# Output projection as split products, y2 reloaded in parts, and half of the last residual on TensorE, in a vision tower kernel on one core

## The chip, the cores and the metric

The kernel runs on one core of a Trainium2 chip. The metric is device time in microseconds of one execution, lower is better; a kernel's time is the median of its runs. The profile shows TensorE (PE, its weight loads PEld), VectorE (DVE), ScalarE (ACT), GpSimd (POOL) and SyncE (SP), which issues most DMAs; ScalarE issues the others. TensorE's clock has two levels here, 1.2 GHz (0.50 in the profile) and 2.4 GHz (1.00).

## The reference

64 images of 3x224x224 are cut into 16x16 patches, 196 tokens each, and embedded to D = 192. The embedding is regrouped for the heads; the rest is one block, all in f32:

```
h   = embed(x)                                       # (64, 196, 192)
q,k,v = silu(h Wq), silu(h Wk), silu(h Wv)           # 12 heads of 16
a   = (q k^T * decay) v ;  a = a * sigmoid(h Wg1 Wg2)
o   = layernorm(a Wo) * ln_w + ln_b
h2  = layernorm(h + o)
xn  = rms_norm(h2) * norm_w ; tok = l2norm(xn) ; sl = l2norm(slots) * scale
L   = sl tok^T ; dispatch = softmax over tokens, combine = softmax over slots
y   = fc2(gelu(fc1(dispatch xn)))                    # 64 slots, each its own 192x768x192
out = layernorm(h2 + combine y)
```

## The kernel before

Two images make an item: NP = 32 items of PT = 392 tokens, in tiles of T = 98 tokens, four a item. There are three stages, each a loop written once for every engine; the engines meet in semaphores alone, and each engine works in program order.

**Stage one, phase1(step)**, runs 34 steps; step i works on the front part of item i (`a`: embedding, q, k, v, gate, scores, values), the middle of item i-1 (`c`: output projection, norms, residual) and the end of item i-2 (`d`: logits, softmaxes, slot inputs, combine weights). The last two steps (NP and NP+1) have no `a`: the drain. Products that need f32 accuracy are done in one of two ways: as plain f32 matmuls (two records each in the profile), or by `product` (L914 to L916) as three matmuls of fp32r operands, each operand split beforehand into a rounded part and the rest. The embedding, q, k and v are split that way; `project_out` (L944) is plain f32 from `og` (attention output times gate, written by VectorE in `gated`, L784) and `wo`. In a step TensorE does embed(i, 0), project_out(i-1, 0), token_features(i-2), embed(i, 1), project_out(i-1, 1), then the rest. VectorE's first_norm starts with bn_stats on the projection's bank (L717). ScalarE starts a step with second_norm (h2, L600), then turned_h (hT, L605, and hTh, L607), and later squares gn into `sq` for a sum (L583). SyncE's step loads the x of item i+2 (after GpSimd's last split of the x before), then stores h2 of item i-2 and the combine weights.

**Stage two, phase2**, runs 32 slot pairs: fc1 (L1191 to L1200), gelu on ScalarE (L636), turns of it (L1209), fc2 (L1178), VectorE's copies hgT (L873) and y2st (L879), ScalarE's store of y2 to DRAM (L643). Six weight buffers are refilled by SyncE as they come free. Behind its last weight loads SyncE issues the first four loads of cbuf (combine weights) and h2r (h2), and then reads y2 back as `y2r`, [128, 32, 192]: rows of slots 0 to 51 of both halves as soon as these are stored, slots 52 to 59 next, slots 60 to 63 last, six DMAs (L377).

**Stage three, phase3**, runs 32 output steps on four sets of buffers (DEEP = 4): GpSimd adds the bias (y2b, L513), TensorE makes four products of 64 rows (L1224) into two PSUM banks, VectorE adds h2r to all four tiles (res, L887), takes statistics (L893, L896), and after GpSimd's power (L508, L510; out_rstd) makes nb3 of the step before (L902, shift); ScalarE writes the four output tiles (L653) from res and issues the store (L656). SyncE reloads cbuf and h2r four steps ahead.

## Time and profile before

| | |
|---|---|
| median of 3 runs | 1304.57 us (1303.42 to 1306.14) |
| the profiled execution's own time | 1307.93 us |
| its span, first to last instruction | 1306.2 us |
| mean granted clock | 0.947 |
| PE busy | 1200.2 us (92%) |
| DVE busy | 782.9 us (60%) |
| ACT busy | 708.3 us (54%) |
| POOL busy | 572.3 us (44%) |
| chain that ended last | PE 74%, DVE 16%, issue 5% |

The shares of busy time are means over the three stages. The page's 40 slices (32.7 us each) show stage one up to slice 30, stage two up to slice 36, and stage three in the last four; the granted clock is below full speed in the first slice, at the change from stage one to stage two, and from the end of stage two on. A busy TensorE is one that has a matmul in flight; ends are modelled.

### The profile page before, as it was taken

How to read it: one execution, taken by the hardware profiler on the slowest of the kernel's cores; microseconds unless marked ns; L12 is line 12 of the kernel's file. 1: busy time of each engine (PE TensorE's matmuls, PEld its weight loads, DVE VectorE, ACT ScalarE, POOL GpSimd, SP SyncE). 2: the span in 40 equal slices, each digit the busy share in tenths (PEclk: the TensorE clock that was granted, in tenths of full speed). 3: DMA queues.
4: the chain of work that ended last, by engine and by line, in shares of the span. 5: the costliest groups of instructions: out<-in, count | busy, mean ns of one | idle time of the engine just before them, and what ended most of it. 6: DMA issues, size and time to landing. Idle time of an engine off the chain costs nothing.

```text
span 1306.2 us, 34037 instructions
## 1 busy us (share of the span) xinstructions
PE 1200.2 (92%) x12578; PEld 962.2 (74%) x12578; DVE 782.9 (60%) x2049; ACT 708.3 (54%) x1613; POOL 572.3 (44%) x878
## 2 busy tenths in 40 slices
PE   5999999999999999999999999999996999995553
PEld 4788888888888888888888888888873555553332
DVE  4566666666666666666666666666673222221797
ACT  5456666666666666666666666666653111110476
POOL 4355454555545554545555455545442000000564
PEclk8999999999999999999999999999995999998655
DMA  4411211111111112111111111121071899995686
GB/s 140 183 39 60 79 61 49 49 49 49 49 49 49 49 57 77 63 49 49 49 49 49 49 49 49 57 78 62 13 270 58 352 422 420 421 389 124 190 263 188
DMA packets 50246, 158.33 MB, mean 121 GB/s; under 512 B 5292, under 2 KB 31266, under 8 KB 37794
## 3 DMA queue, kind: packets, MB, share of 16 engines
q1 hardware_dynamic: 32610, 145.04, 30.9%
q10 hardware_dynamic: 17600, 12.78, 3.2%
q8 instruction: 26, 0.43, 0.1%
q14 instruction: 10, 0.08, 0.0%
HBM read 132.18 MB, written 25.62 MB: 121 GB/s over the span
## 4 chain that ended last, share of the span: by engine, by line
PE 74%; DVE 16%; issue 5%; ACT 1%; POOL 1%; DVEq 1%; SPq 1%; DMA 0%; ACTq 0%; POOLq 0%
PE ps L914 9%; PE ps L915 8%; PE ps L916 7%; DVE p_sb L778 7%; PE ps L973 7%; PE ps L944 6%; PE ps L1008 6%; PE ps L1178 5%; PE ps L1195 4%; PE ps L1051 3%; PE ps L956 3%; PE ps L957 2%; DVE res L887 2%; PE ps L991 2%; PE ps L1074 2%
## 5 line engine op out<-in xcount | busy, mean ns | idle before, releaser
L413 POOL TENSOR_TENSOR xl<-x_sb,xh 128x392 fp32r<-128x392 f32 x192 | 189.1, 1019 | 86.6 <-DVE gn L753 78.7
L778 DVE TENSOR_TENSOR p_sb<-ps,dec 98x1176 f32<-98x1176 f32 x128 | 177.0, 1383 | 56.4 <-PE ps L973 56.4
L973 PE MATMUL ps<-qm,kT 32*98 32x196 f32 x1536 | 117.0, 343 | 9.7 <-DVE p_sb L778 7.6
L717 DVE BATCH_NORM_STATS2 st<-ps 98x6 f32<-98x192 f32 x128 | 40.0, 355 | 130.8 <-PE ps L944 130.8
L1008 PE MATMUL ps<-p_sb,vpad 98*32 98x98 f32 x3072 | 112.7, 251 | 1.5 <-DVE p_sb L778 1.5
L636 ACT ACTIVATE hg<-ps 128x768 f32<-128x768 f32 x32 | 26.0, 812 | 159.0 <-PE ps L1200 159.0
L1008 PEld LDWEIGHTS ps<-p_sb,vpad 98*32 98x32 f32 x3072 | 84.7, 109 | 35.0 <-issue 24.6
L973 PEld LDWEIGHTS ps<-qm,kT 32*98 32x98 f32 x1536 | 75.2, 158 | 35.2 <-DVE p_sb L778 23.1
L944 PE MATMUL ps<-wo,og 96*98 96x192 f32 x512 | 93.7, 325 | 0.0
L879 DVE COPY y2st<-ps 128x192 f32<-128x192 f32 x32 | 11.4, 358 | 136.1 <-PE ps L1178 128.7
L1224 PE MATMUL ps<-y2b,cbuf 64*98 64x192 f32 x256 | 48.2, 526 | 44.6 <-POOL y2b L513 44.6
L653 ACT ACTIVATE o_sb<-res,nb,rstd 98x192 f32<-98x192 f32 x128 | 59.6, 536 | 54.4 <-DVE nb L902 53.7
L944 PEld LDWEIGHTS ps<-wo,og 96*98 96x98 f32 x512 | 83.2, 164 | 0.9
L457 POOL TENSOR_TENSOR invn<-nrm,expo 98x4 f32<-98x4 f32 x32 | 32.4, 1011 | 117.6 <-DVE nrm L763 117.6
L914 PE MATMUL ps<-xl,wh 128*128 128x392 f32 x192 | 70.3, 366 | 11.8 <-POOL xl L413 11.8
L500 POOL CAST pickb<-pick 128x128 fp32r (+1 forms) x32 | 9.4, 293 | 162.4 <-PE ps L1200 162.4
L443 POOL TENSOR_TENSOR qd<-qs,qdec 96x196 f32<-96x196 f32 x64 | 36.0, 563 | 100.3 <-ACT qs L569 100.3
L432 POOL TENSOR_TENSOR hTl<-hT,hTh 128x392 fp32r<-128x392 f32 x32 | 32.6, 1018 | 104.1 <-ACT hTh L607 104.1
L540 ACT ACT_TABLE_LOAD x60 | 77.0, 1283 | 1.1
L1224 PEld LDWEIGHTS ps<-y2b,cbuf 64*98 64x98 f32 x256 | 32.0, 262 | 60.6 <-issue 49.5
L1178 PEld LDWEIGHTS ps<-w2v,hgT 128*64 128x64 f32 x768 | 53.2, 139 | 29.2 <-issue 18.5
L1178 PE MATMUL ps<-w2v,hgT 128*64 128x192 f32 x768 | 70.9, 335 | 3.8 <-DVE hgT L873 3.8
(175 smaller groups left out, 3390.4 us busy)
## 6 DMA issues: line engine op xcount, KB each, us to landing
x_sb<-in_xT SPq DMA_DIRECT2D x32, 1176.0 KB, 5.7
w1v<-in_fc SPq DMA_DIRECT2D x32, 1152.0 KB, 8.2
w2v<-in_fc SPq DMA_DIRECT2D x32, 1152.0 KB, 10.8
h_dram<-h SPq DMA_DIRECT2D x32, 294.0 KB
h2r<-h_dram SPq DMA_DIRECT2D x32, 294.0 KB
out<-o_sb ACTq DMA_DIRECT2D x32, 294.0 KB
comb_dram<-cst SPq DMA_DIRECT2D x32, 98.0 KB, 1.8
cbuf<-comb_dram SPq DMA_DIRECT2D x32, 98.0 KB, 4.0
```

What stands on the lines that cost most here:

```text
L413: pool.tensor_tensor(xl[:, k], x_sb[:, k], xh[:, k].bitcast(F32), ALU.subtract)\
L540: act.activation(warm[:, 1:2], warm[:, 0:1], func)
L653: act.activation(o_sb[:, n, t], res[:, n, t], ACT.Identity, bias=nb3[:, n, t:t + 1], scale=rstd3[:, n, t:t + 1]).then_inc(o_rdy, 1)
L778: dve.tensor_tensor(dst, src, rate.unsqueeze(2).to_broadcast([T, PAIRS, 2, TOK]), ALU.mult)\
L914: pe.matmul(out, hi, x_lo, start=start, stop=False)
L915: pe.matmul(out, lo, x_hi, start=False, stop=False)
L916: return pe.matmul(out, hi, x_hi, start=False, stop=stop)
L944: mm = pe.matmul(ps[0:T, 2 + x, (t % 2) * D:(t % 2) * D + D], og[0:G, k, t * T:(t + 1) * T], wo[0:G, k], start=(k == 0), stop=(k == 1))
L973: mm = pe.matmul(ps[0:T, SC_AT + r, mt * TOK:(mt + 1) * TOK].rearrange("p (b n) -> p b n", b=2), kT[rows, g, n], qm[rows, g, :, n], start= ...
L1008: mm = pe.matmul(ps[32 * b:32 * b + 32, 5 + g, a * TOK + mt * T:a * TOK + mt * T + T], vpad[:, 2 * a + mt, 32 * (g * HG + h):32 * (g * HG ...
L1178: mm = pe.matmul(ps[64 * s:64 * s + 64, 4 + n % 2, 0:D], hgT[:, k, at:at + 64], w2v[n][:, s, k], start=(k == 0), stop=(k == FJ - 1))
L1224: mm = pe.matmul(ps[0:T, 2 * n + a, k * D:(k + 1) * D], cbuf[64 * a:64 * a + 64, n, k * T:(k + 1) * T], y2b[64 * a:64 * a + 64, n, :], sta ...
```

## The change

- `project_out` becomes a `product`: ScalarE rounds `og` to `ogh` in two copies at the very start of its step (ahead of second_norm), VectorE makes `ogl` = og - ogh in two subtractions ahead of first_norm, and TensorE waits for ogl. `wo` is split once at the start (`woh`, `wol`), one VectorE instruction more. `wo`'s buffer goes into the region that the weight buffers reuse.
- The squares of gn go into h2 (in steps with `a`) or hb instead of a tile of their own; ScalarE waits for the h2 store before that, and SyncE stores h2 ahead of loading x.
- In the drain TensorE does products whose result nobody reads (`idle_products`, f32, 128x128 by 128 columns): 8 ahead of project_out, then 12, 16 and 2 in step NP, and 6, 2, 4 and 2 in step NP+1. 24 more stand behind the last fc2.
- y2 is read back only after all its stores, in parts by item: items 0 to 3, 4 to 11 and 12 to 31, each as two DMAs of 64 partitions. GpSimd makes the first four y2b after the first part, then waits for the others.
- In an output step TensorE first puts h2r of tiles 0 and 1 into PSUM by a product with the identity (98 rows, 384 columns), and the products of these tiles accumulate on it. VectorE adds h2r for tiles 2 and 3 alone, takes statistics of tiles 0 and 1 from PSUM, and ScalarE reads these two tiles from PSUM. TensorE therefore waits for o_sb of four steps before.

```diff
-READY = (NU - RING, NU - REST, NU)
+PARTS = ((0, DEEP), (DEEP, 3 * DEEP), (3 * DEEP, NP))
@@ SyncE
             def step(i, d):
+                if d:
+                    store_h2(i - 2)
                 load_x(i + 2)
                 if d:
-                    store_h2(i - 2)
                     store_comb(i - 2)
...
-            sp.wait_ge(fc2_mm, RING * TURNS - 2)
-            for u0, u1 in zip((0,) + READY[:-1], READY):
-                for m in range(Y2):
-                    sp.wait_ge(y2_stored[m], 16 * ((u1 - m + Y2 - 1) // Y2))
+            for m in range(Y2):
+                sp.wait_ge(y2_stored[m], 16 * ((NU - m + Y2 - 1) // Y2))
+            for (p0, p1), there in zip(PARTS, y2r_loaded):
                 for a in range(2):
-                    rows = slice(64 * a + 2 * u0, 64 * a + 2 * u1)
-                    sp.dma_start(y2r[rows, :, :], y2_dram[2 * u0:2 * u1, a]).then_inc(y2r_loaded, 16)
+                    sp.dma_start(y2r[64 * a:64 * a + 64, p0:p1, :], y2_dram[:, a, p0:p1, :]).then_inc(there, 16)
@@ GpSimd
-            pool.wait_ge(y2r_loaded, 32 * len(READY))
+            pool.wait_ge(y2r_loaded[0], 32)
             for n in range(DEEP):
                 bias(n, n)
+            for there in y2r_loaded[1:]:
+                pool.wait_ge(there, 32)
@@ ScalarE
             def step(i, a, c, d, d_before, more):
+                if c:
+                    for g in range(2):
+                        act.wait_ge(og_sb, 2 * i - 1 + g)
+                        act.activation(ogh[:, g], og[:, g], ACT.Copy).then_inc(ogh_rdy, 1)
                 if d:
                     second_norm(i - 2)
...
                 if c:
+                    squares = h2 if a else hb
+                    if a and not (isinstance(i, int) and i == 1):
+                        act.wait_ge(h2_stored, 16 * (i - 1))
...
                 for t in range(4):
-                    act.activation(o_sb[:, n, t], res[:, n, t], ACT.Identity,
+                    src = ps[0:T, 2 * n, t * D:(t + 1) * D] if t < 2 else res[0:T, n, t - 2]
+                    act.activation(o_sb[:, n, t], src, ACT.Identity,
@@ VectorE
-            dve.tensor_scalar(wo[0:G], wo[0:G], 0.5, None, ALU.mult).then_inc(wo_halved, 1)
+            dve.tensor_scalar(woh[:, :, :], wo[:, :, :], 0.5, None, ALU.mult).then_inc(wo_halved, 1)
+            dve.wait_ge(wo_halved, 1)
+            dve.scalar_tensor_tensor(wol[:, :, :], wo[:, :, :], 0.5, woh[:, :, :].bitcast(F32),
+                                     ALU.mult, ALU.subtract).then_inc(wo_halved, 1)
...
                 if c:
+                    for g in range(2):
+                        dve.wait_ge(ogh_rdy, 2 * i - 1 + g)
+                        dve.tensor_tensor(ogl[:, g], og[:, g], ogh[:, g].bitcast(F32), ALU.subtract)\
+                            .then_inc(ogl_rdy, 1)
                     first_norm(i - 1, 0)
...
-                dve.tensor_tensor(res[0:T, n].rearrange("p (x t) d -> p x (t d)", x=2),
-                                  ps[0:T, 2 * n:2 * n + 2, 0:2 * D],
-                                  h2r[:, n].rearrange("p (x t) d -> p x (t d)", x=2), ALU.add)\
-                    .then_inc(res_rdy, 1)
+                dve.tensor_tensor(res[0:T, n].rearrange("p t d -> p (t d)"), ps[0:T, 2 * n + 1, 0:2 * D],
+                                  h2r[:, n, 2:4].rearrange("p t d -> p (t d)"), ALU.add).then_inc(res_rdy, 1)
+                for t in range(2):
+                    dve.bn_stats(st3[:, n, t, :], ps[0:T, 2 * n, t * D:(t + 1) * D])
                 dve.wait_ge(res_rdy, p + 1)
-                for t in range(4):
-                    dve.bn_stats(st3[:, n, t, :], res[0:T, n, t])
+                for t in range(2):
+                    dve.bn_stats(st3[:, n, 2 + t, :], res[0:T, n, t])
@@ TensorE
+            def idle_products(bank, count):
+                for _ in range(count):
+                    pe.matmul(ps[:, bank, 0:128], ident[:, :], ident[:, :], start=True, stop=True)
...
-                pe.wait_ge(og_sb, 2 * j + 2)
+                pe.wait_ge(ogl_rdy, 2 * j + 2)
                 for t in (2 * x, 2 * x + 1):
                     for k in range(2):
-                        mm = pe.matmul(ps[0:T, 2 + x, (t % 2) * D:(t % 2) * D + D],
-                                       og[0:G, k, t * T:(t + 1) * T], wo[0:G, k], start=(k == 0), stop=(k == 1))
+                        n = slice(t * T, (t + 1) * T)
+                        mm = product(ps[0:T, 2 + x, (t % 2) * D:(t % 2) * D + D],
+                                     ogh[:, k, n], ogl[:, k, n], woh[:, k], wol[:, k], k == 0, k == 1)
...
                 if c:
+                    if not a:
+                        idle_products(0, 8)
                     project_out(i - 1, 0)
...
+                    if not a and not c:
+                        idle_products(0, 6)
                     logits(i - 2)
...
                 if d and not a:
+                    idle_products(0, 12 if c else 2)
                     logits_turned(i - 2)
...
+                    else:
+                        idle_products(0, 16 if c else 4)
                     dispatch_turned(i - 2)
+                    if not a:
+                        idle_products(0, 2)
...
             pe.wait_ge(hgT_rdy, NU)
+            idle_products(6, 24)
             def out_step(p, n, w):
+                if not at_start(w):
+                    pe.wait_ge(res_rdy, p + 1 - DEEP)
+                    pe.wait_ge(o_rdy, 4 * (p + 1 - DEEP))
+                pe.wait_ge(h2r_loaded[n], 16 * w + 16)
+                pe.matmul(ps[0:T, 2 * n, 0:2 * D], ident[0:T, 0:T], h2r[:, n, 0:2].rearrange("p t d -> p (t d)"),
+                          start=True, stop=False)
                 pe.wait_ge(cbuf_loaded[n], 16 * w + 16)
                 pe.wait_ge(y2b_rdy, p + 1)
-                if not at_start(w):
-                    pe.wait_ge(res_rdy, p + 1 - DEEP)
-                for t in range(4):
+                for t in (2, 3, 0, 1):
                     a, k = t // 2, t % 2
                     mm = pe.matmul(ps[0:T, 2 * n + a, k * D:(k + 1) * D],
                                    cbuf[64 * a:64 * a + 64, n, k * T:(k + 1) * T],
-                                   y2b[64 * a:64 * a + 64, n, :], start=True, stop=True)
+                                   y2b[64 * a:64 * a + 64, n, :], start=(a == 1), stop=(t != 0))
```

## Rows read from the trace of the kernel before

**Rows 1.** Busy time by stretch; the columns stand in the first line.
```profile
core 0: us, PE busy (x) PEld busy (x) DVE busy (x) ACT busy (x) POOL busy (x), PEclk, DMA share, GB/s
100.00:500.00 400.00, 394.97 (x4502) 340.96 (x4500) 267.18 (x675) 257.84 (x597) 204.73 (x292) 1.00 0.17 56
975.00:980.00 5.00, 2.29 (x22) 2.15 (x20) 4.41 (x16) 0.50 (x1) 3.87 (x8) 0.94 1.02 418
985.00:1006.50 21.50, 16.33 (x76) 9.46 (x76) 4.56 (x15) 8.35 (x23) 5.03 (x12) 0.50 0.08 25
1005.00:1010.00 5.00, 4.07 (x24) 1.58 (x24) 0.47 (x1) 0.81 (x1) 0.47 (x2) 0.83 0.00 0
1160.00:1165.00 5.00, 5.00 (x42) 2.46 (x40) 1.32 (x2) 0.31 (x1) 0.17 (x1) 1.00 1.02 422
1180.00:1190.00 10.00, 10.00 (x87) 5.45 (x85) 1.55 (x3) 1.62 (x2) 0.00 (x0) 1.00 0.82 190
1190.00:1200.00 10.00, 4.59 (x32) 3.16 (x30) 1.58 (x3) 0.00 (x0) 0.00 (x0) 0.83 0.43 87
1240.00:1260.00 20.00, 11.99 (x62) 7.36 (x58) 18.64 (x74) 14.47 (x32) 13.67 (x23) 0.50 0.87 260
```
**Rows 2.** Timeline, steady item: start, duration (us), engine, line, what; [idle before <-releaser].
```profile
851.99 0.56 DVE L784 SCALAR_TENSOR_TENSOR og<-gt,ps 96x392 f32<-96x392 f32 x1 [1.37 <-PE ps L1019]
852.76 0.52 ACT L629 ACTIVATE yT<-ps 128x128 f32 x2
855.71 1.32 PEld L944 LDWEIGHTS ps<-wo,og 96*98 96x98 f32 x8
856.08 0.50 ACT L605 ACTIVATE hT<-ps 128x392 f32<-128x392 f32 x1 [0.88 <-PE ps L916]
857.38 0.63 DVE L717 BATCH_NORM_STATS2 st<-ps 98x6 f32<-98x192 f32 x2 [4.17 <-PE ps L944]
...
885.66 1.32 PEld L944 LDWEIGHTS ps<-wo,og 96*98 96x98 f32 x8
```
**Rows 3.** Timeline, end of stage two; last, how long y2's stores take to land.
```profile
1187.97 2.17 PE L1178 MATMUL ps<-w2v,hgT 128*64 128x192 f32 x24
...
1193.50 0.36 DVE L879 COPY y2st<-ps 128x192 f32<-128x192 f32 x1 [7.41 <-DMA y_dram<-y2st]
...
1194.77 3.64 PE L1178 MATMUL ps<-w2v,hgT 128*64 128x192 f32 x24 [3.83 <-DVE hgT L873]
...
DMA to landing us min/median/max: 1.6/7.6/20.3
```
**Rows 4.** Timeline, the drain of stage one.
```profile
973.99 0.63 DVE L717 BATCH_NORM_STATS2 st<-ps 98x6 f32<-98x192 f32 x2 [1.10 <-PE ps L944]
...
980.39 0.92 PE L1059 MATMUL ps<-ident,Lt 98*64 98x98 f32 x8 [3.11 <-DVE Lt L791]
...
985.31 0.66 PE L1066 MATMUL ps<-ident,Es 128*98 128x128 f32 x2 [4.00 <-ACT Es L611]
...
992.48 2.92 PE L1051 MATMUL ps<-slT,tokT 96*98 96x64 f32 x16 [1.46 <-ACT tokT L556]
```
**Rows 5.** Timeline, stage three: two of VectorE's sums, three of ScalarE's output groups.
```profile
1218.61 1.86 ACT L653 ACTIVATE o_sb<-res,nb,rstd 98x192 f32<-98x192 f32 x4 [29.69 <-DVE nb L902]
...
1245.16 0.96 DVE L887 TENSOR_TENSOR res<-ps,h2r 98x768 f32<-98x768 f32 x1 [0.29 <-issue]
...
1287.94 0.96 DVE L887 TENSOR_TENSOR res<-ps,h2r 98x768 f32<-98x768 f32 x1 [0.28 <-issue]
...
1298.49 1.86 ACT L653 ACTIVATE o_sb<-res,nb,rstd 98x192 f32<-98x192 f32 x4 [0.67 <-DVE nb L902]
...
1301.03 1.86 ACT L653 ACTIVATE o_sb<-res,nb,rstd 98x192 f32<-98x192 f32 x4 [0.67 <-ACT o_sb L653]
```
**Rows 6.** Timeline, V's first and last product and a rounding copy, steady item.
```profile
856.61 0.53 ACT L607 ACTIVATE hTh<-hT 128x392 fp32r<-128x392 f32 x1
...
866.00 0.25 PE L914 MATMUL ps<-wvl,hTh 128*98 128x192 f32 x1
...
868.04 0.25 PE L916 MATMUL ps<-wvh,hTh 128*98 128x192 f32 x1
```

More of the change, by code:

```diff
@@ L46 @@
 DEEP = 4
-REGION = 34704
+REGION = 34048
 EARLY = 4
@@ L135, in vit_tower @@
         bst = place("bst", [128, F])
-        wvst = place("wvst", [128, 2, D])
+        wvst, wo = place("wvst", [128, 2, D]), place("wo", [G, 2, D])
         dist, steps = place("dist", [T, T]), place("steps", [G, T])
@@ L157, in vit_tower @@
         y2b = place("y2b", [128, DEEP, D])
-        res, o_sb = place("res", [T, DEEP, 4, D]), place("o_sb", [T, DEEP, 4, D])
-        og = sb("og", [G, 2, PT])
+        res, o_sb = place("res", [T, DEEP, 2, D]), place("o_sb", [T, DEEP, 4, D])
+        og, ogh, ogl = sb("og", [G, 2, PT]), sb_r("ogh", [G, 2, PT]), sb_r("ogl", [G, 2, PT])
+        woh, wol = sb_r("woh", [G, 2, D]), sb_r("wol", [G, 2, D])
         hb = sb("hb", [T, 4, D])
@@ L164, in vit_tower @@
         gn = sb("gn", [T, 4, D])
-        sq = sb("sq", [T, 4, D])
         h2 = sb("h2", [T, 4, D])
@@ L168, in vit_tower @@
         tokT = sb("tokT", [G, 2, PT])
-        wo = sb("wo", [G, 2, D])
         slT = sb("slT", [G, 2, S])
@@ L218, in vit_tower @@
         val_mm, pv_mm, og_sb = sem("val_mm"), sem("pv_mm"), sem("og_sb")
+        ogh_rdy, ogl_rdy = sem("ogh_rdy"), sem("ogl_rdy")
         wo_mm = sem("wo_mm")
@@ L240, in vit_tower @@
         h2r_loaded = [sem(f"h2r_loaded{n}") for n in range(DEEP)]
-        y2r_loaded = sem("y2r_loaded")
+        y2r_loaded = [sem(f"y2r_loaded{n}") for n in range(len(PARTS))]
         cbuf_loaded = [sem(f"cbuf_loaded{n}") for n in range(DEEP)]
@@ L334, in _ @@
             store_comb(NP - 4)
+            store_h2(NP - 3)
             sp.wait_ge(hT_mm, 2 * NP)
@@ L339, in _ @@
             load_weights(1, 1)
-            store_h2(NP - 3)
             sp.wait_ge(sc_mm, 4 * NP)
@@ L580, in step @@
                 if c:
+                    squares = h2 if a else hb
+                    if a and not (isinstance(i, int) and i == 1):
+                        act.wait_ge(h2_stored, 16 * (i - 1))
                     for t in range(4):
                         act.wait_ge(gn_rdy, 4 * (i - 1) + t + 1)
-                        act.activation(sq[:, t], gn[0:T, t], ACT.Square, accum_out=ss[:, t:t + 1]).then_inc(ss_rdy, 1)
+                        act.activation(squares[0:T, t], gn[0:T, t], ACT.Square, accum_out=ss[:, t:t + 1]).then_inc(ss_rdy, 1)
                 if a:
@@ L1111, in step @@
                         pe.wait_ge(w_split, 12)
-                        pe.wait_ge(wo_halved, 1)
+                        pe.wait_ge(wo_halved, 2)
                         slots_turned()
```

## The prediction

> **What bounds the kernel now.** I read the page first for the split into stages, then the granted clock and engine shares by stretch, then one item's timeline in each stage. The first stage (items through attention, about 0 to 1002 us) takes three quarters of the time. There TensorE is busy 98.7% at full clock while VectorE stands at 67% [rows 1], so TensorE's own order of work sets the pace: one item every 29.95 us (the output projection's first weight load starts at 855.71 and, an item later, at 885.66) [rows 2]. The second stage (32 slot pairs, to about 1190) is again TensorE back to back [rows 1]. Between the stages lie two places where TensorE waits: the end of the second stage, where it works 4.59 of 10 us and then nothing until 1211 [rows 1, 3], and before that the drain of the first stage at the 1.2 GHz level [rows 1, 4]. The third stage (32 output steps, from 1211) has TensorE at 1.2 GHz and 60% busy, VectorE at 93%, ScalarE at 72% [rows 1]; its step is 2.67 us ((1287.94 - 1245.16) / 16) [rows 5].
>
> **Output projection (project_out).** Before, half an item's projection is 8 records in 1.32 us, 2.60 an item (0.163 a record) [rows 2]. After, it is 24 split products like those of V, which have the same 192 columns and 98 weight columns: 24 start between 866.00 and 868.04, 0.089 us apart, so 2.13 us an item [rows 6]. Both halves stand on the chain. The gain is 0.47 us for each of items 0 to 30, 14.6 us, if what feeds it is on time. What feeds it: ScalarE now rounds og in two copies, VectorE subtracts in two. By the like forms a copy takes 0.53 us [rows 6] and a subtraction 0.56, as og itself [rows 2]. The last og of an item is ready at 852.55, ScalarE is free at 853.28 after its yT copies [rows 2]; the copies end near 854.3, the subtractions near 854.9, while the projection's turn is at 855.71: 0.8 us to spare. VectorE was idle for 4.17 us there, so its 1.1 us costs nothing. ScalarE's h2, four instructions between yT and hT, moves back by 1 us to end at 856.2, and hT, which started at 856.08 after waiting 0.88 us, starts 0.1 us later [rows 2]; GpSimd's next steps move by 0.2 us and VectorE keeps 0.9 us of slack before zs. I cost that at nothing. With the cover gone, each microsecond by which the subtraction is late costs 31 us. The h2 store moves ahead of the x load on SyncE: the store then lands long before h2 is used as scratch for the squares, and the x load still waits for the same split; nothing on either side of the path. At the start VectorE makes one more 96x384 product (the 0.56 us of og's form, plus its wait) ahead of the slots and of hTl, behind which the first projections stand: +0.6 us, with nothing and 0.7 as the ends. Stage one: -14.0.
>
> **The drain, with the idle products.** The last item has no embedding to hide the new copies. og(31) is there at 972.36 and ScalarE free at 972.98; two copies and two subtractions in file end near 974.6, against 972.41 for the start before; the first half is 0.24 shorter, so VectorE's chain, which runs from 973.99 on through Lt to Es, is 1.9 us later [rows 4]. Against that stands the clock. TensorE is at 1.2 GHz from about 979.4 (0.94 of a stretch in which it works 2.29 of 5 us) up to about 1006.7 (0.83 of the stretch in which stage two has begun) [rows 1]. An idle product is two records of 128 columns; 192 columns take 0.165 [rows 2], so one takes 0.22 us at full clock and 0.44 at half. Groups of 8, 12 and 16 take 1.8, 2.6 and 3.5 us; the holes are 2.2 (new), 3.1 and 4.0 us [rows 4]. So they fit at full clock and leave holes of about 1 us, and I expect the clock to stay at 2.4 GHz. At full clock TensorE's pieces shrink: the logits of item 31 from 2.92 to about 1.5, the dispatch turn from 0.66 to 0.4 [rows 4]. From 985 to 1006.5 TensorE works 16.3 us at the low level [rows 1]; halved that is 8.2, of which 2.5 lie beside other work (the turns of gn behind ScalarE's h2, the turned logits behind VectorE's chain, weight loads that don't halve), so 5.7 come back: 1.3 before the logits of item 31, 1.4 in them, 1.2 behind them and 1.8 in the first slot pair. Drain: +1.9 - 5.7 = -3.8.
>
> **The reload of y2.** Before, most of y2 was read back beside the last slot pairs; the y2 stores queue behind it, VectorE waits 7.41 us for one, and the last fc2 products start at 1194.77 and run 3.64 us; the pair before took 2.17, and its pitch of 5.85 would put them at 1192.0, where hgT is due [rows 3]. With no read beside them, the last products end near 1194.2, the last store is issued at 1194.7 and lands about 2.2 us later (stores take 1.6 to 20.3, and 7.6 in the middle, mostly beside the weights) [rows 3]: 1196.9. Now comes what the change pays: all of y2, 3.15 MB (128 x 32 x 192 numbers of 4 bytes), is read after that. GpSimd starts the first four biases after the first eighth, but then waits for all the rest before out_rstd(0), and without rstd(0) neither nb3(0) nor the first output instruction exists: VectorE stands in step 1. So what counts is the end of the whole reload. The bound from below is the weights' rate, 422 GB/s: 7.5 us. The bound from above is what the old reload of 52 rows had, 190 GB/s: 16.6 us [rows 1]. I take 200, as the new transfers too cover only half of the partitions at a time, with 16 shares in place of 13: 15.7 us. The Trainium skill (SBUF — State Buffer, "Door 1: The DMA port swizzle" and "Can I just issue two DMAs to hit both halves?") says that 64 partitions reach eight of sixteen ports, 196 GB/s measured for 1 MiB, and that two transfers to the two halves go one after the other; by it the reload is estimated at 16 us. The trace agrees, with its 190 GB/s. With 1.4 us of latency the reload ends at 1196.9 + 1.4 + 15.7 = 1214.0, rstd(0) comes 1.3 later, and the first output instruction at 1215.6, against 1218.61 [rows 5]. That is -3.0. The 24 idle products before it (5.3 us) end before the first bias, cost nothing, and bring nothing: TensorE does four steps, then waits for o_sb of step 0 until about 1217, and after such waits the clock has stood at 1.2 GHz (0.83 already in the stretch with 4.59 of 10 us) [rows 1].
>
> **The output step.** VectorE's sum takes 0.96 of its step for 768 columns; with 384 it saves 0.4 (og has 392 and takes 0.56): 2.2 to 2.3 are left [rows 2, 5]. But ScalarE does not get faster by this. Its four instructions take 1.86, and then 0.67 pass with its own completion, the store's issue and the waits, even for the last step, where no engine held it up but itself: 1298.49 to 1301.03 is 2.54 [rows 5]. Two of its four now read PSUM; reading it costs 0.02 to 0.04 less (a 392-column copy 0.50 from PSUM, 0.53 from SBUF) [rows 2, 6]. So 2.47, plus a loop's turn every fourth step (0.28 before VectorE's sum at 1287.94; on ScalarE unseen, 0 to 0.3) [rows 5]: 2.55 us against 2.66 (82.4 us from 1218.61 to 1301.03 over 31 steps), -3.4. TensorE gets one product of 384 columns: 0.65 us at 2.4 GHz (as two products of 192 in the projection), 1.30 at 1.2 [rows 2], beside 1.3 at 1.2 for the four others (11.99 us for 62 records between 1240 and 1260, eight a step, their tail taken off) [rows 1]: 2.6 us a step, 1.3 at full clock, plus 0.2 to 0.3 of waits and load. At the slow level that would pass ScalarE's step, but then TensorE is busy all the time, as it was before the clock rose at 1006.7 [rows 1]; the four buffers cover such stretches.
>
> **The sum.** -14.0 -3.8 -3.0 -3.4 = -24.2 us. The profiled execution had 1307.93 us (span 1306.20), 3.4 above the median of 1304.57; taken off the median it gives 1280.4. Between the bounds the main case runs from 1275 to 1285.
>
> **Rivals.**
> (a) The reload at the weights' rate, both halves in flight together: 7.5 instead of 15.7 us, 1272. For it: six transfers are queued at once, on all 16 engines; against it: the 190 GB/s of a queued pair. 0.13.
> (b) TensorE takes VectorE's place in the output steps, since a rise of the clock does not come or is lost again at once: 2.85 us a step, 31 x 0.3 = +9.3, 1290. For it: the clock stood at 1.2 GHz through the whole stage before [rows 1]; against it: TensorE then worked 60% of the time, and would now work without a break. 0.15.
> (c) The clock falls in the drain all the same: the groups of 12 and 16 then take 5.3 and 7.0 us, 2.2 and 3 us longer than their holes, and the 5.7 us of shrunk pieces don't come: +10.9, 1291. 0.06.
> (d) VectorE was the only brake in the third stage, ScalarE follows it to 2.3 us: another -7.8, 1272.6. Against it stands the last step's 2.54 [rows 5]. 0.05.
> (e) Slower than before: the new wait of project_out is reached before its operand, in every item, as in the drain. If ScalarE's copies come only behind h2 or yT, the 2.2 us of the drain show in each item too; less the 0.47 that makes +1.7 x 31 = 54, with the rest 1348. It decides for slower once the subtraction is 0.8 us (the cover) + 0.8 (24.2 / 31) late, beyond 857.3. The order of the code speaks against it. 0.04.
> (f) The projection's gain is taken up by other waits of the item (VectorE's slack before decay and zs is 1 us): -14.6 gone, 1295. 0.05.
>
> **How the numbers follow.** The main case has 0.52. The range takes in the main case, (a), (b), and (d): 1270 to 1291, with most of (c). The measurement can tell 0.2%, 2.6 us, from no change; every case but (e) is faster by more than that. Faster 0.94, same 0.02, slower 0.04.
>
> **What would show it.** The item's pitch in stage one 29.5 instead of 29.95, and no wait of TensorE before the projection; full clock from 975 to 1180; the last y2 copy without a wait on DMA; the end of the reload some 15 us after its first issue, and GpSimd's long wait on it after four biases; ScalarE's output instructions 2.5 us apart with no wait for nb3 to speak of. The prediction is wrong if the reload takes 8 us, if output steps are paced by TensorE at 1.2 GHz, or if the projection waits for the subtraction.

## The result, and the profile of the changed kernel

The changed kernel takes 1286.54 us (median, 1284.25 to 1289.56), the kernel before, run beside it, 1305.24: a ratio of 0.986, 95% interval 0.9835 to 0.9885, so 18.7 us less. The profiled execution has 1287.57 us and a span of 1285.8 (before 1307.93 and 1306.20), 20.4 less. The prediction was 1280.4: right in its sign and inside its range of 1270 to 1291, but 6.1 us too low and outside its main case, 1275 to 1285.

Where the 20.4 us went shows when the two traces are laid side by side at four points. Each row is a difference between starts; the third column is what the sum had for that part.

| part, and the instruction that ends it | before, after | change | predicted |
|---|---|---|---|
| items of stage one: first product of the last item's second embedding | 947.66, 931.94 | -15.7 | -14.0 |
| drain: second slot pair's first product | 1009.25, 989.75 | -3.8 | -3.8 |
| stage two's end and the reload: first output instruction | 1218.61, 1196.41 | -2.7 | -3.0 |
| 31 output steps: last output group | 1301.03, 1280.76 | +1.9 | -3.4 |

Three parts came within 1.7 us of the forecast. The fourth has the other sign, and its 5.3 us are the miss. (Of the 6.1 us by which the median misses, 0.7 are the starting point: the prediction took off 1304.57, the kernel before has 1305.24 here.) The stretches of the changed kernel, with the columns as in [rows 1]:
```profile
core 0: us, PE busy (x) PEld busy (x) DVE busy (x) ACT busy (x) POOL busy (x), PEclk, DMA share, GB/s
100.00:500.00 400.00, 395.57 (x4656) 342.97 (x4655) 287.61 (x726) 276.48 (x637) 208.21 (x298) 1.00 0.16 54
...
985.00:990.00 5.00, 4.06 (x25) 1.75 (x25) 0.00 (x0) 2.02 (x2) 0.47 (x2) 1.00 0.04 13
1180.00:1190.00 10.00, 6.72 (x43) 3.34 (x41) 3.99 (x18) 0.00 (x0) 2.23 (x4) 1.00 1.02 227
1190.00:1200.00 10.00, 1.67 (x4) 0.55 (x6) 4.02 (x17) 2.86 (x7) 5.00 (x9) 0.60 0.72 177
1200.00:1210.00 10.00, 10.00 (x36) 5.01 (x38) 6.54 (x35) 6.15 (x15) 5.75 (x11) 0.50 0.86 240
...
1220.00:1240.00 20.00, 15.28 (x71) 7.39 (x72) 15.27 (x78) 14.00 (x33) 14.25 (x25) 0.83 0.89 280
1240.00:1260.00 20.00, 20.00 (x74) 9.13 (x74) 14.08 (x71) 11.71 (x28) 11.39 (x21) 0.58 0.87 232
```
Against [rows 1]: stage one is as full as it was, with two copies and two subtractions more per item on ScalarE and VectorE. At 985 us TensorE is at full clock, where it was at 0.50. In the third stage, between 1240 and 1260 us, VectorE has come down from 18.64 of 20 us to 14.08, and the full engine is now TensorE: 20.00 of 20, at a clock of 0.58.

A steady item, the answer to [rows 2]: two embeddings 29.46 us apart (before 29.95), the copies of og, the subtractions, and the projection's first product.
```profile
838.57 0.45 PE L934 MATMUL ps<-xl,wh 128*128 128x392 f32 x1
839.36 0.95 ACT L554 ACTIVATE ogh<-og 96x392 fp32r<-96x392 f32 x2
839.93 1.04 DVE L829 TENSOR_TENSOR ogl<-og,ogh 96x392 fp32r<-96x392 f32 x2 [0.70 <-ACT ogh L554]
840.22 1.85 ACT L608 ACTIVATE h<-t,mur,ra 98x192 f32<-98x192 f32 x4
841.89 0.25 PE L934 MATMUL ps<-wol,ogh 96*98 96x192 f32 x1
...
868.03 0.45 PE L934 MATMUL ps<-xl,wh 128*128 128x392 f32 x1
```
The subtractions end at 840.97, 0.9 us ahead of the projection, and it doesn't wait. The end of stage two and the reload, the answer to [rows 3]:
```profile
1172.50 2.17 PE L1208 MATMUL ps<-w2v,hgT 128*64 128x192 f32 x24 [1.05 <-DVE hgT L889]
1174.79 0.36 DVE L895 COPY y2st<-ps 128x192 f32<-128x192 f32 x1 [2.34 <-PE ps L1208]
1176.87 3.70 SPq L376 DMA_DIRECT2D y2r<-y_dram  x6
1180.90 2.23 POOL L512 TENSOR_TENSOR y2b<-y2r,b 128x192 f32<-128x192 f32 x4 [23.49 <-DMA y2r<-y_dram]
1182.71 0.35 SPq L353 DMA_DIRECT2D cbuf<-comb_dram  x1
1194.50 0.20 POOL L507 TENSOR_TENSOR ve<-mv,expo 98x4 f32<-98x4 f32 x1 [11.37 <-DMA y2r<-y_dram]
1196.41 0.91 ACT L662 ACTIVATE o_sb<-ps,nb,rstd 98x192 f32<-98x192 f32 x2 [26.99 <-DVE nb L918]
```
VectorE's wait for a y2 store is gone, the last products take 2.17 us in place of 3.64, and GpSimd stands for the rest of the reload behind its four biases: 17.6 us from the first issue. From 1182.71 on the next loads of cbuf and h2r are under way beside it. And the output steps, at 1.2 GHz (three lines) and at 2.4 GHz (four):
```profile
1201.39 1.60 PE L1253 MATMUL ps<-h2r,ident 98*98 98x384 f32 x2
1202.92 1.61 PE L1259 MATMUL ps<-y2b,cbuf 64*98 64x192 f32 x8
1204.46 1.60 PE L1253 MATMUL ps<-h2r,ident 98*98 98x384 f32 x2
...
1223.17 0.89 PE L1253 MATMUL ps<-h2r,ident 98*98 98x384 f32 x2 [0.67 <-ACT o_sb L662]
1223.79 0.91 ACT L662 ACTIVATE o_sb<-ps,nb,rstd 98x192 f32<-98x192 f32 x2 [0.67 <-ACT o_sb L662]
1223.99 0.90 PE L1259 MATMUL ps<-y2b,cbuf 64*98 64x192 f32 x8
1226.25 0.51 ACT L662 ACTIVATE o_sb<-ps,nb,rstd 98x192 f32<-98x192 f32 x1 [0.67 <-ACT o_sb L662]
```
At 1.2 GHz a step of TensorE is 3.07 us (1201.39 to 1204.46), back to back. At 2.4 GHz it has 1.66 us of work and ScalarE sets the pace: 2.46 us (1223.79 to 1226.25), its wait being for its own end.

### The profile page after: what moved, and what is told of

Same layout as the page of the kernel before. It is cut to its first block, busy times and chain, and to the rows that moved or that the text cites. A ratio compares the mean times of both kernels' runs of the same rounds, so it can differ in the third digit from the quotient of the medians.

```text
span 1285.8 us, 35236 instructions
## 1 busy us (share of the span) xinstructions
PE 1221.5 (95%) x13050; PEld 965.5 (75%) x13050; DVE 801.5 (62%) x2114; ACT 732.8 (57%) x1677; POOL 571.9 (44%) x878
## 4 chain that ended last, share of the span: by engine, by line
PE 81%; DVE 12%; ACT 2%; issue 2%; DMA 1%; SPq 1%; ACTq 0%; POOL 0%; DVEq 0%; POOLq 0%
PE ps L934 11%; PE ps L935 10%; PE ps L936 10%; DVE p_sb L790 7%; PE ps L994 7%; PE ps L1029 6%; PE ps L1208 5%; PE ps L1225 4%; PE ps L1072 3%; PE ps L977 3%; PE ps L978 3%; PE ps L1012 2%; PE ps L1230 2%; PE ps L1239 2%; PE ps L1095 2%; PE ps L1253 2%
## 5 line engine op out<-in xcount | busy, mean ns | idle before, releaser
L895 DVE COPY y2st<-ps 128x192 f32<-128x192 f32 x32 | 11.4, 358 | 131.4 <-PE ps L1208 131.4
L541 ACT ACT_TABLE_LOAD x60 | 77.0, 1283 | 1.1
L546 ACT ACTIVATE xh<-x_sb 128x1176 fp32r<-128x1176 f32 x64 | 71.7, 1168 | 0.6 <-DMA x_sb<-in_xT 0.6
L977 PE MATMUL ps<-xl,whl 128*128 128x392 f32 x192 | 68.0, 354 | 0.0
L480 POOL TENSOR_TENSOR xn<-gn,ra 98x192 f32<-98x192 f32 x128 | 67.9, 559 | 0.0
L748 DVE SCALAR_TENSOR_TENSOR t<-t,rstd,hb 98x192 f32<-98x192 f32 x128 | 60.4, 512 | 11.3 <-POOL rstd L463 11.2
L935 PE MATMUL ps<-xh,wl 128*128 128x392 f32 x192 | 66.9, 348 | 0.0
```

The costliest lines, as they stand in the source:

```text
L480: pool.tensor_tensor(xn[0:T, t], gn[0:T, t], amp[:, t:t + 1].to_broadcast([T, D]), ALU.mult)\
L541: act.activation(warm[:, 1:2], warm[:, 0:1], func)
L546: act.activation(xh[:, c], x_sb[:, c], ACT.Copy).then_inc(xh_rdy, 1)
L935: pe.matmul(out, lo, x_hi, start=False, stop=False)
L977: pe.matmul(ps[:, 1, 0:PT], whl[:, k], xl[:, k], start=(k == 0), stop=False)
```

## The experiments

Theory A: the output steps are paced by TensorE whenever it is at 1.2 GHz, and that turns -3.4 into +1.9. Rival B: something else makes the slow steps (loads, stores, the new reads of PSUM). Each kernel was timed against the kernel before on the same chip. Because earlier parts vary by 1 to 3 us between executions, the table gives beside the median what the trace shows of the third stage alone: the start of ScalarE's first output group and the length from there to the last (31 steps).

| kernel | median us | ratio, 95% | first group | 31 steps | a step |
|---|---|---|---|---|---|
| changed kernel | 1286.54 | 0.986 (0.9835-0.9885) | 1196.41 | 84.35 | 2.72 |
| old_step | 1288.94 | 0.9868 (0.9849-0.9888) | 1199.22 | 82.43 | 2.66 |
| one_tile | 1282.55 | 0.9827 (0.9812-0.9841) | 1198.01 | 79.13 | 2.55 |
| alternate | 1286.48 | 0.9852 (0.9834-0.987) | 1199.43 | 83.70 | 2.70 |
| hot | 1282.4 | 0.982 (0.9805-0.9835) | 1200.48 | 77.59 | 2.50 |
| warm_start | 1286.64 | 0.9847 (0.9827-0.9868) | 1199.84 | 80.69 | 2.60 |
| hot_sp | 1298.82 | 0.9946 (0.9931-0.996) | 1197.19 | 95.33 | 3.08 |
| hot_sp2 | 1281.9 | 0.9814 (0.9795-0.9833) | 1197.88 | 77.88 | 2.51 |
| only_projection | 1295.01 | 0.9921 (0.9907-0.9934) | 1205.67 | 82.40 | 2.66 |
| no_drain_idle | 1293.38 | 0.9909 (0.9895-0.9923) | 1203.10 | 83.44 | 2.69 |
| four_stores | 1282.28 | 0.9817 (0.9804-0.9831) | 1191.34 | 84.35 | 2.72 |
| best | 1281.17 | 0.9809 (0.9789-0.9828) | 1193.34 | 86.03 | 2.78 |
| short_fill | 1278.88 | 0.9793 (0.978-0.9807) | 1192.14 | 79.62 | 2.57 |

**The old output step in the changed kernel.** TensorE's product with ident is out, `res` has four tiles again:
```
-pe.matmul(ps[0:T, 2 * n, 0:2 * D], ident[0:T, 0:T], h2r[:, n, 0:2].rearrange("p t d -> p (t d)"),
-          start=True, stop=False)
...
-dve.tensor_tensor(res[0:T, n].rearrange("p t d -> p (t d)"), ps[0:T, 2 * n + 1, 0:2 * D],
-                  h2r[:, n, 2:4].rearrange("p t d -> p (t d)"), ALU.add).then_inc(res_rdy, 1)
+dve.tensor_tensor(res[0:T, n].rearrange("p (x t) d -> p x (t d)", x=2), ps[0:T, 2 * n:2 * n + 2, 0:2 * D],
+                  h2r[:, n].rearrange("p (x t) d -> p x (t d)", x=2), ALU.add).then_inc(res_rdy, 1)
...
```


> The changed kernel with the output step of before (VectorE adds h2 to all four tiles, TensorE has its four products only, ScalarE reads res); projection, reload and unused products stay as changed. Theory A: the changed output steps lose time because TensorE, at 1.2 GHz for two thirds of them, needs 3.07 us a step and paces them (mean 2.72); taken off TensorE, VectorE paces as before at 2.66: about 1285, 1.9 us less than the changed kernel. Rival B: the slow steps come from something that the step of before has as well (loads of h2 and the combine weights, stores of the output); then VectorE's 0.4 us more a step comes on top: 3 to 9 us more than the changed kernel.


```profile
1220.00:1240.00 20.00, 12.59 (x64) 7.88 (x62) 18.67 (x76) 13.89 (x30) 13.26 (x23) 0.50 0.87 261
```
The stage is that of before: VectorE 18.67 of 20 us, TensorE 12.59 at 0.50, 82.43 us for the 31 steps, 1.9 less than with the new step, as theory A has it, and not 3 to 9 more. The other traces repeat it: with the step of before and no fillers the 31 steps take 82.40 (only_projection) and 82.42 (the kernel before), with the new one 83.44 to 84.35 (no_drain_idle, alternate, four_stores and the changed kernel). The new step is therefore no gain by itself. The median shows nothing of this: 1288.94 where 1285 was expected, 2.4 above the changed kernel and not below it, with ratios whose intervals overlap; this trace begins its third stage 2.8 us later for a reason told below. Theory A rests here on the traces alone.

**One tile on TensorE in place of two.**
VectorE's sum has three tiles (576 columns, laid side by side in PSUM), TensorE's product one (192):
```
-pe.matmul(ps[0:T, 2 * n, 0:2 * D], ident[0:T, 0:T], h2r[:, n, 0:2].rearrange("p t d -> p (t d)"),
-          start=True, stop=False)
+pe.matmul(flat[0:T, n, FLAT[0]:FLAT[0] + D], ident[0:T, 0:T], h2r[:, n, 0], start=True, stop=False)
...
```


> The changed kernel, but TensorE adds h2 to one tile of four (192 columns) instead of two, VectorE to three. Theory A: TensorE's step at 1.2 GHz is 3.07 - 0.77 = 2.30 us, VectorE's 2.3 + 0.2 = 2.5, ScalarE's 2.46: 2.5 us a step at either clock, 31 x 0.2 = 6 to 7 us less than the changed kernel, about 1280. Rival B (TensorE isn't what makes the slow steps): no gain, -1 to +3.


```profile
1220.00:1240.00 20.00, 19.55 (x80) 11.27 (x80) 17.41 (x79) 14.08 (x32) 13.84 (x23) 0.50 0.87 272
...
1240.37 0.76 DVE L905 TENSOR_TENSOR res<-ps,h2r 98x576 f32<-98x576 f32 x1 [0.22 <-PE ps L1259]
1240.63 0.95 PE L1254 MATMUL ps<-h2r,ident 98*98 98x192 f32 x2 [0.41 <-ACT o_sb L664]
1243.67 0.51 ACT L664 ACTIVATE o_sb<-ps,nb,rstd 98x192 f32<-98x192 f32 x1 [0.67 <-ACT o_sb L664]
```
At the same 0.50 the product of 192 columns takes 0.9 us in place of 1.53. TensorE no longer paces, and ScalarE waits for itself again. The step is 2.55 us, nearly all of it at the low clock. The transfers are the same as in the changed kernel, so they don't make the slow steps. (ScalarE reads one tile from PSUM here, not two; that its reads don't make them either is shown by the run with a full clock below.) 1282.55 is 4.0 below the changed kernel, where 6 to 7 were expected; by the stage it is 5.2. Its 79.13 us are 3.3 below the kernel before: with half of the work moved, the stage gives the 3.4 that was forecast for all of it.

**Another order of the four products**: `for t in (2, 0, 3, 1)`.

> The changed kernel, but the four combine products of an output step in the order 2, 0, 3, 1 instead of 2, 3, 0, 1, so that neighbours use different halves of the rows. If TensorE paces the slow steps (theory A) and products in the two halves overlap (four of 192 columns take 0.84 us where one of 384 takes 0.81), the four shrink at 1.2 GHz from 1.53 to about 1.3 us: 0.2 x 18 slow steps, 3 to 4 us less. If TensorE doesn't pace, or order doesn't matter: 0.


```profile
1254.14 1.60 PE L1259 MATMUL ps<-y2b,cbuf 64*98 64x192 f32 x8
1255.67 1.60 PE L1253 MATMUL ps<-h2r,ident 98*98 98x384 f32 x2
```
A miss: the four products still take 1.53 us. Order does nothing, so an overlap of neighbours in the two halves of the rows, which I had supposed, doesn't show (see the last section).

**TensorE kept busy.** 49 unused products in the wait for the reload, and three in each step from the fifth on:
```
+if at_start(w) and n == DEEP - 1:
+    idle_products(6, 49)
...
+if not at_start(w):
+    for _ in range(3):
+        mm = pe.matmul(ps[:, 2 * n, 2 * D:BANK], ident[:, :], ident[:, :], start=True, stop=True)
 mm.then_inc(cmb_mm, 1)
```


> The changed kernel with 49 more unused products of 128 columns while TensorE waits for the reload (10.84 us), and three in each output step from the fifth on (0.66 us at full clock, in the 0.8 us that TensorE has left there). Theory A with a clock that holds as long as TensorE has no holes: 2.4 GHz through the whole stage, ScalarE paces at 2.53: 31 x 0.19 = 6 us less, about 1280. Rival C: the clock falls although TensorE works without a break, as it did near 1233 us; then a step takes 3.07 + 1.32 = 4.4 us in those stretches and the kernel is 15 to 25 us slower.


```profile
1220.00:1240.00 20.00, 19.51 (x129) 12.58 (x128) 16.07 (x80) 14.27 (x32) 14.01 (x25) 1.00 0.89 281
...
1242.79 0.91 ACT L662 ACTIVATE o_sb<-ps,nb,rstd 98x192 f32<-98x192 f32 x2 [0.68 <-ACT o_sb L662]
1245.25 0.91 ACT L662 ACTIVATE o_sb<-ps,nb,rstd 98x192 f32<-98x192 f32 x2 [0.67 <-ACT o_sb L662]
```
The clock stays at 2.4 GHz, rival C falls, and with the same real work, reads of PSUM included, the stage takes 77.59 us, 6.8 less: 2.50 us a step, ScalarE's 2.46 and a loop's turn every fourth. This is the run in which only TensorE's clock and its fillers differ from the changed kernel; with old_step and one_tile it settles theory A. The median is 4.1 lower, not 6; this trace begins the stage 4.1 us late. Of that, 2.9 are told below, and 1.1 is a longer reload (GpSimd waits 12.42 us for its end, 11.4 to 12.4 in the other traces with the same transfers).

**Only the fillers ahead of the steps** (49, none in the steps):

> The changed kernel with the 49 unused products in the wait for the reload alone, none in the output steps. Theory: the clock is at 2.4 GHz when the steps begin, but at that clock TensorE has 1.66 us of work in a step of 2.46, and as near 1233 us it falls after some steps: 5 or 6 steps at 2.46 instead of 3.07, 3 to 4 us less than the changed kernel, about 1283. Rival: the level at the start decides for the stage, then it is as good as with unused products in each step: 1281 or less. Other rival: it falls at once, no gain.


```profile
1200.00:1215.00 15.00, 11.15 (x68) 5.52 (x68) 13.60 (x67) 11.26 (x26) 12.26 (x20) 1.00 0.80 250
1220.00:1240.00 20.00, 20.00 (x69) 9.50 (x68) 12.32 (x62) 12.59 (x30) 11.14 (x20) 0.50 0.85 239
1250.00:1270.00 20.00, 13.45 (x81) 6.60 (x80) 16.66 (x83) 14.27 (x32) 14.85 (x25) 1.00 0.90 279
```
The steps begin at full clock, where TensorE works 11.15 of 15 us; then the clock falls, TensorE works 20.00 of 20, and only after some 24 us does it rise (0.93 between 1210 and 1220, 0.94 between 1240 and 1260). The level at the start doesn't decide for the stage. The stage is 3.7 us shorter, as expected, though the median shows none of it: 1286.64, where 1283 was expected.

**The output stores on SyncE**, to free ScalarE from waiting for its own end (with the fillers in each step). First the store of step p ahead of the next loads:
```
 load_h2(p + DEEP, n)
+sp.wait_ge(o_rdy, 4 * p + 4)
+sp.dma_start(out_v[p], o_sb[:, n]).then_inc(out_stored[n], 16)
...
```


> As the run with three unused products in each output step (TensorE at 2.4 GHz through the whole stage, 2.50 us a step, ScalarE pacing), and the output store issued by SyncE behind ScalarE's four instructions, so that ScalarE neither waits for its own end nor issues. Theory: the 0.67 us between two groups of ScalarE shrinks to 0.1, VectorE (2.28 us busy) or TensorE with the unused products (2.32) paces at 2.35 to 2.4: 31 x 0.12 = 3 to 5 us less than that run, about 1278. Rival: SyncE's stores stand in the way of its loads, or the gap of ScalarE is a wait for VectorE or GpSimd in other clothes: no gain, up to 3 us more.


```profile
1235.00 0.36 SPq L353 DMA_DIRECT2D cbuf<-comb_dram  x1
1235.54 0.58 SPq L356 DMA_DIRECT2D h2r<-h_dram  x1
1236.80 0.86 PE L1259 MATMUL ps<-h2r,ident 98*98 98x384 f32 x2 [0.94 <-DMA h2r<-h_dram]
1237.01 0.36 SPq L385 DMA_DIRECT2D out<-o_sb  x1
```
A clear miss, 16 us more than with the stores on ScalarE (3.08 us a step): SyncE waits for the end of ScalarE's step before it asks for the h2 that TensorE needs five steps on, and TensorE waits for that load. Then the same with the store one step later, behind the loads:

> The run with SyncE's stores again, but the store of step p-1 stands behind the loads of step p instead of that of step p ahead of the loads of p+1. Theory: in the run before, SyncE waited for ScalarE's end of step p before it asked for h2 of step p+5, and that round trip (load 4.2 us, TensorE 2.4, VectorE 2.3, GpSimd 1.3, ScalarE 1.8, waits, over 5 steps) made 3.1 us a step; with the stores one step later no load waits for ScalarE: VectorE or TensorE with its unused products paces at 2.35 to 2.4, about 4 us less than the run with stores on ScalarE, near 1278. Rival: SyncE's issues are too slow or the stores collide with the loads in its queue: 2.6 us or more a step, 1285 and up.


```profile
1237.89 0.91 ACT L674 ACTIVATE o_sb<-ps,nb,rstd 98x192 f32<-98x192 f32 x2 [0.54 <-DVE nb L928]
1238.42 0.25 PEld L1265 LDWEIGHTS ps<-h2r,ident 98*98 98x98 f32 x2 [0.70 <-ACT o_sb L674]
```
The detour is gone, but no gain is left: 2.51 us a step, as with the stores on ScalarE, and 1281.9, where 1278 was expected. ScalarE now waits for VectorE's nb, and TensorE for ScalarE's end of four steps ago; many steps take 2.3, others 2.8 to 3.3. I read that as the ring of four buffers (TensorE, VectorE, GpSimd's rstd, VectorE's nb behind its next step, ScalarE, and back), which takes four steps' time, 10.0 us. The fillers are in this ring too: VectorE waits for the last of the three, which ends 0.9 us behind the real products (1235.53 and 1234.66 in the step ahead of the rows). So that the ring paces is argued, not shown; more buffers, or the semaphore ahead of the fillers, would tell, and neither was tried (four sets of buffers take all eight banks of PSUM). Rival (d) of the prediction, 2.3 us a step, didn't come true here with ScalarE relieved, but a run with ScalarE relieved, a full clock and no fillers doesn't exist.

**The first stage's change alone**, in the kernel before:

> The kernel before with the change of the first stage alone: split operands of the output projection, the copies and subtractions that make them, the h2 store ahead of the x load. Drain, reload and output steps are those of before, no unused products. Theory: 31 x 0.47 = 14.6 us less in the items, 0.6 more at the start, 1.9 more in the drain, where the copies are not hidden: about 1293, ratio 0.991. Rival: the move of the reload or the output step gave part of the change's gain up to the first output instruction: then this gives 9 us or less.

1295.01 against 1306.37 beside it: 11.4 less, ratio 0.9921 against the 0.991 expected. The last item's second embedding starts at 933.52, 14.1 earlier than before; the drain then takes 3.7 us more, not 1.9. The projection carries by itself over half of the whole gain.

**No unused products in the drain:**

> The changed kernel without the unused products in the drain (the 24 ahead of the output steps stay). Theory: TensorE falls to 1.2 GHz in the drain as before and stays there until stage two has begun: 3 to 6 us more than the changed kernel, about 1291. Rival: the unused products only fill holes, and the drain is set by VectorE and ScalarE: 0 to 1 us more, or up to 1 less, since no group of them is in the way.


```profile
985.00:990.00 5.00, 3.77 (x18) 2.14 (x20) 0.19 (x2) 2.53 (x6) 1.45 (x5) 0.50 0.06 20
```
The clock is at 0.50 as before. The median is 6.8 us higher than that of the changed kernel, the ratio 0.9909 against 0.986; 3 to 6 were expected. From the last embedding to the last products of stage two this trace has 246.9 us (931.55 to 1178.41), the changed kernel 240.6: 6.3 us, all of it before the second slot pair.

**The reload over all 128 partitions.** y2 in DRAM as [2, S, NP, D], each y2 store in four pieces of 32 rows:
```
-for a in range(2):
-    sp.dma_start(y2r[64 * a:64 * a + 64, p0:p1, :], y2_dram[:, a, p0:p1, :]).then_inc(there, 16)
+sp.dma_start(y2r[:, p0:p1, :], y2_all[:, p0:p1, :]).then_inc(there, 16)
...
```


> The changed kernel with y2 in DRAM laid out with the half a ahead of the slot, so that each eighth, quarter and rest of the reload is one transfer over all 128 partitions instead of two over 64; each y2 store of stage two becomes four of 32 rows. Theory A (a transfer over 64 partitions runs at some 200 GB/s, and two of them don't run side by side): the reload takes 7.5 to 9 us instead of 17.6 from its first issue: 7 to 9 us less, about 1279; three more issues a slot pair on ScalarE (0.1 us each) are hidden there. Rival B: the rate of the reload is that of its many small pieces in DRAM or of the queue: same time, up to 2 us more for the four stores at the end.


```profile
1180.00:1190.00 10.00, 6.75 (x43) 3.35 (x41) 3.99 (x18) 0.00 (x0) 2.72 (x6) 1.00 1.00 368
...
1178.12 1.28 SPq L376 DMA_DIRECT2D y2r<-y_dram  x3
1189.43 0.20 POOL L507 TENSOR_TENSOR ve<-mv,expo 98x4 f32<-98x4 f32 x1 [5.58 <-DMA y2r<-y_dram]
```
The reload takes 11.3 us from its first issue in place of 17.6. For its 3.15 MB that is 279 GB/s in place of 179; the stretch shows 368 in place of 227, but this counts the loads of cbuf and h2r that run beside it as well. The first output group is 5.1 us earlier and the median 4.3 lower, where 7 to 9 were expected: 11.3 us is more than the 9 I had allowed, and behind four issues a store the reload starts later (1178.12 against 1176.87). The Trainium skill (SBUF — State Buffer, "Can I just issue two DMAs to hit both halves?") says that two transfers to the two halves of the partitions serialize, and that only one transfer over all 128 reaches all sixteen ports. These two runs agree, with 17.6 and 11.3 us; the layout of y2 in DRAM and the number of stores changed with it, while the pieces of a row stayed as long (3 to 15 KB).

**All together, twice.** First with 49 fillers ahead of step 3:

> All together: unused products in the output steps, stores of the output by SyncE one step late, y2 laid out so that the reload is three transfers over 128 partitions, and seven more unused products at the start of stage two. Expected: 6 us less than the run before by the reload, 1 to 3 less by a clock that stays up near 985 us: about 1270. If the gains overlap (the reload being no longer what the first output step waits for): 1275.


```profile
1190.69 11.72 PE L943 MATMUL ps<-ident 128*128 128x128 f32 x98
1202.25 0.81 PE L1271 MATMUL ps<-h2r,ident 98*98 98x384 f32 x2
...
1203.95 0.56 DVE L916 TENSOR_TENSOR res<-ps,h2r 98x384 f32<-98x384 f32 x1 [8.62 <-PE ps L1277]
```
A clear miss: 1281.17, where 1270 was expected, or 1275 if the gains overlap. The reload now ends at 1191, while the fillers, counted for the long one, hold step 3 back to 1202: VectorE waits 8.62 us for it. Fillers that outlast the wait they fill cost what they run over. With 20 there, 30 instead of 24 ahead of the steps, and the output stores back on ScalarE:

> The changed kernel with the reload as three transfers over 128 partitions (four stores a slot pair), three unused products in each output step from the fifth on, seven at the start of stage two, 30 instead of 24 ahead of the output steps and 20 instead of 49 ahead of the fourth step; the output stores stay on ScalarE. Theory: in the run with all together the 49 unused products ran 10 us past the end of the shorter reload and kept the products of step 3 back (ScalarE's third group 10 us late); with 20 they fit into the 5 us that TensorE waits, both gains add up: first output instruction near 1192, 31 steps in 77.6 us, about 1274. Rival: the clock falls in the hole ahead of the first bias (1.66 us there) and the steps run at 1.2 GHz with 4.4 us each for a while: 1285 or more.


```profile
1190.22 0.20 POOL L507 TENSOR_TENSOR ve<-mv,expo 98x4 f32<-98x4 f32 x1 [6.76 <-DMA y2r<-y_dram]
...
1194.06 1.34 PE L1261 MATMUL ps<-h2r,ident 98*98 98x384 f32 x2 [1.76 <-ACT o_sb L665]
```
1278.88, the lowest here: ratio 0.9793, 7.7 us below the changed kernel and 26.9 below the kernel before. It missed its 1274 by 4.9. One step still ran at 1.2 GHz behind the 1.76 us hole, and the stage took 79.62 us, not 77.6: 2.0 of it. The rest lies in the sum itself: 1192 and 77.6 and the 7.1 us from the start of the last output group to the end of the execution make 1276.7.

## Why the prediction was right, and where it was not

**Stage one** held: an item is 0.49 us shorter (0.47 predicted), and the cover of the subtraction is 0.9 us (0.8). The 15.7 us at the last embedding hold some 1.4 us of luck. The traces fall into two groups by the granted clock of their first 100 us, 0.95 or 0.97. The kernel before is in the first; the seven others there (old_step, one_tile, alternate, hot, warm_start, only_projection, best) come to the last embedding at 933.1 to 933.5, 14.1 to 14.5 ahead. The profiled execution and the five others at 0.97 come there at 931.6 to 932.4. Like against like, -14.0 is right.

**The drain** held in its sum, -3.8, not in its parts. Without fillers it grew by 2.5 (no_drain_idle) and 3.7 (only_projection) to the second slot pair, where 1.9 was predicted; against no_drain_idle the fillers give 6.3, where 5.7 was. Two terms were too small, and the errors cancel. What I had not seen is that it is near an edge. In four traces of the same instructions (old_step, alternate, hot, warm_start) the clock falls once more at 985 to 990 (0.66 to 0.68), and stage two's last products start 242.1 us after the last embedding; in the others (the changed kernel, one_tile, hot_sp, hot_sp2, and four_stores with its other stores) they start 240.6 after it. The row of hot:
```profile
985.00:990.00 5.00, 4.15 (x15) 1.40 (x15) 0.00 (x0) 2.16 (x5) 0.22 (x2) 0.66 0.08 23
```
So 1.5 us come and go with the execution, and with the 1.4 of the start they are the 2.9 us by which hot begins late. They may also be why the median gained less (18.7 us) than the profiled execution (20.4); but the profiled execution of before was itself 2.7 us above its median, and the executions without a trace don't tell. Rival (c) is true in small. short_fill has seven more products there and shows 5.00 of 5 us busy at 1.00.

**The reload** ran as worked out: 17.6 us from the first issue, where 1.4 and 15.7 were taken (no row gives the 1.4). Over the 17.6 us it ran at 179 GB/s, less than half of the weights' 422, so rival (a) fell, and four_stores turned the same reason round. Its gain of 2.7 (3.0 predicted) holds against the profiled execution of before. From the second slot pair to the first output group that has 209.4 us, the changed kernel 206.7, but only_projection, with the old reload, 206.9: there the wait of VectorE for a y2 store was 6.30 us and the last products took 2.17. The nine traces with the reload moved as in the changed kernel have 206.7 to 207.8. So the old reload costs up to 3 us more in one trace and nothing in the other, and the moved one is about even with its better case: that -2.7 came near the forecast is in part luck of the execution profiled before. The 24 fillers ahead of the steps weren't tried alone.

**The output step** failed, and in one step of it. ScalarE's pace of 2.47 and 2.55 with loop turns was right: 2.46 and 2.50 in the run with a full clock. VectorE's busy time fell by 0.47 us a step (18.64 of 20 us at 2.66 a step, 16.07 of 20 at 2.50), where 0.4 was worked out. The step that failed is "the four buffers cover such stretches", with the figure before it. TensorE's step at 1.2 GHz was put at 2.6 us plus 0.2 to 0.3; it is 3.07, since both the 384 columns (1.30 predicted) and the four products (1.3) take 1.53. And the claim that the clock comes back when TensorE "is busy all the time" rested on one case, the first slot pairs; here it worked 10.00 of 10 us from 1200 on at 0.50, and between 1240 and 1260 20.00 of 20 at 0.58. Four buffers cover the first two or three steps of a slow stretch, not those behind them. Of the 31 steps ten have 2.95 us or more (3.07 in the mean), the other 21 take 2.56 in the mean, where 2.55 was predicted. Ten times 0.52 is 5.2, and with the 0.01 of the others it is the 5.3 that are missing. The prediction itself had named output steps paced by TensorE at 1.2 GHz as a sign that it is wrong; for a third of the steps it is. This is rival (b), in mechanism and in price: it put 2.85 on every step and 1290 on the whole, and the kernel lies between it and the main case. It had 0.15 and deserved more, since [rows 1] showed the whole stage at 0.50, and the change put 1.5 us on the engine that is slow there while it took 0.4 off the other.

## What to carry to other kernels

Before work is moved to TensorE, cost it at the clock that the trace shows in that stage, and let it rise only where a row shows it rise under the same load; a step that is free at 2.4 GHz can be the longest at 1.2. A smaller share (one tile of four) kept the gain at the low clock, and three unused products a step kept the clock, but fillers must end before the wait that they fill. And where a queue works in order, a wait placed ahead of a load is a wait of everyone who needs the load.

## What the runs showed of the hardware

- TensorE back to back doesn't mean full clock: in the output steps of the changed kernel it stayed at 1.2 GHz for 17 to 24 us with no hole, and it then fell again when it was at 2.4 GHz with 1.66 us of work in 2.46. With the fillers (hot) it held 2.4 GHz at 19.5 of 20 us.
- A product over 64 rows costs half of one over 98 for the same columns, in f32: four of 192 columns take 1.53 us at 1.2 GHz, one of 384 over 98 rows takes 1.53 too. The order of the halves doesn't matter. Why is open.
- Reading back the 3.15 MB of y2, beside other loads, took 11.3 us in transfers over 128 partitions and 17.6 us in pairs of transfers over 64 (four_stores and the changed kernel).
